# A wide causal attention phase whose mask and scale move to VectorE, and whose exponentials are eight per item on ScalarE with their sums

## The reference

```python
q = split_heads(x @ Wq)
k = split_heads(x @ Wk)
v = split_heads(x @ Wv)
q = apply_rope(q)
k = apply_rope(k)
sim = jnp.einsum('bid,bjd->bij', q, k) * scale
causal = jnp.tril(jnp.ones((t, t), dtype=bool))
sim = jnp.where(causal[None], sim, -jnp.inf)
attn = jax.nn.softmax(sim, axis=-1)
out = jnp.einsum('bij,bjd->bid', attn, v)
...
return out @ Wo + bo
```

## Time and profile before

| | |
|---|---|
| median of 3 runs | 1160.22 us (1157.81 to 1162.24) |
| the profiled execution | 1151.02 us, of which the span of the engines is 1149.2 us |
| wide attention phase in the span | about 594 to 1002 us |
| one block of it, at steady pace | 24.12 us, so 6.03 us an item |

### The profile page before, as it was taken

The page is one execution under the profiler, slowest core; times in us unless marked ns, Lnnn a source line. Parts: engine busy times, 40 slices in busy tenths (PEclk is TensorE's granted clock), DMA queues, the critical chain, the costliest instruction groups (busy, mean ns, idle before and its releaser), DMA issues. The chain is left out here.

```text
span 1149.2 us, 38657 instructions
## 1 busy us (share of the span) xinstructions
PE 993.0 (86%) x14756; PEld 799.4 (70%) x14759; DVE 846.6 (74%) x2027; ACT 588.4 (51%) x982; POOL 562.9 (49%) x705
## 2 busy tenths in 40 slices
PE   5999999999945799999937999999999999778554
PEld 2666666667632799999936888888888888655113
DVE  5878787888749344444418989999999998578676
ACT  3665656677730566666612444444444444366545
POOL 4232424353300533333126888888888877433104
PEclk9999999999965899999968999999999999955555
DMA  8200000000000111111130000000000000050002
GB/s 257 101 2 0 2 11 20 21 20 28 11 28 0 45 47 48 48 46 48 39 108 13 12 13 11 9 11 11 11 11 9 11 9 1 11 138 20 1 0 74
DMA packets 36984, 37.60 MB, mean 33 GB/s; under 512 B 7142, under 2 KB 31145, under 8 KB 36522
## 3 DMA queue, kind: packets, MB, share of 16 engines
q1 hardware_dynamic: 31690, 27.33, 7.9%
q0 software_dynamic: 4352, 8.92, 3.1%
q10 hardware_dynamic: 866, 0.33, 0.1%
HBM read 27.65 MB, written 8.91 MB: 32 GB/s over the span
## 5 line engine op out<-in xcount | busy, mean ns | idle before, releaser
L1283 POOL DMA_INDIRECT e_x<-xn_rows,e_where x72 | 68.2, 947 | 162.5 <-DVE e_where L1264 114.7
L360 POOL TENSOR_SCALAR n_KX<-n_KT,n_of_head 128x512 f32<-128x512 f32 x124 | 83.8, 697 | 122.1 <-ACT n_KT L601 85.2
L1253 DVE COPY e_y<-e_Y_ps 128x128 f32<-128x128 f32 x72 | 21.0, 292 | 112.5 <-PE e_Y_ps L1220 112.5
L760 DVE TENSOR_REDUCE n_row_max<-n_S_ps 128x16 f32<-128x1024 f32 x64 | 78.1, 1221 | 26.3 <-PE n_S_ps L451 26.3
L1440 POOL TENSOR_TENSOR a_E<-a_E,a_rsum 128x512 f32<-128x512 f32 x64 | 66.6, 1041 | 53.8 <-DVE a_rsum L1804 53.7
L665 ACT ACTIVATE n_ET<-n_ET_ps 128x1024 f32<-128x1024 f32 x64 | 65.5, 1023 | 46.5 <-PE n_ET_ps L461 45.8
L461 PEld LDWEIGHTS n_ET_ps<-ident,n_E 128*128 128x128 f32 x512 | 57.1, 142 | 34.9 <-issue 20.1
L764 DVE TENSOR_TENSOR n_E<-n_S_ps,n_row_max 128x1024 f32<-128x1024 f32 x64 | 78.4, 1225 | 2.9
L1210 PE MATMUL e_G_ps<-e_xT,e_gate_here 128*128 128x128 f32 x576 | 77.2, 278 | 0.0
L1210 PE MATMUL e_U_ps<-e_xT,e_up_here 128*128 128x128 f32 x576 | 76.9, 277 | 0.0
L1688 ACT ACTIVATE a_OT<-a_VQ_ps 128x512 f32<-128x512 f32 x64 | 38.2, 597 | 75.4 <-PE a_VQ_ps L1584 75.4
(11 more groups left out here) (280 smaller groups left out, 2674.3 us busy)
## 6 DMA issues: line engine op xcount, KB each, us to landing
slot_out<-e_y SPq DMA_DIRECT2D x72, 64.0 KB, 1.5
X<-in_x SPq DMA_DIRECT2D x8, 256.0 KB, 5.4
n_ctxT<-in_ctxT SPq DMA_DIRECT2D x8, 256.0 KB, 3.2
m_gate_w<-in_L_ffn_gate_w SPq DMA_DIRECT2D x1, 2048.0 KB, 7.4
m_up_w<-in_L_ffn_up_w SPq DMA_DIRECT2D x1, 2048.0 KB, 13.4
m_down_w<-in_L_ffn_down_w SPq DMA_DIRECT2D x1, 2048.0 KB, 17.7
xn_rows<-n_xn SPq DMA_DIRECT2D x8, 256.0 KB, 2.2
t_ctxT<-in_ctxT SPq DMA_DIRECT2D x8, 256.0 KB, 3.4
```

What stands on the lines that cost most here:

```text
L360: last = nc.gpsimd.tensor_scalar(KX[:, p, :, h * T:(h + 1) * T], src, of_head[:, h:h + 1], 1.0, ALU.mult, ALU.mult)
L760: nc.vector.tensor_reduce(row_max[:, u % 2, :], src, AX.X, ALU.max).then_inc(max_done, 1)
L1283: nc.gpsimd.indirect_dma_start(out=x[:, j, :], out_offset=None, in_=k.xn_rows, in_offset=bass.IndirectOffsetOnAxis(ap=where[:, j, :], axis ...
```

## The change

It does this in the wide attention phase alone:

- The eight constant matmuls are gone. VectorE multiplies the scores by 1/8 and adds a constant tile `future` (0 or -1e30) in one instruction (`mask_scores`, scalar_tensor_tensor) from PSUM into E, and then takes the negated row maximum `low` from E.
- ScalarE takes the exponentials in eight instructions per item, one for each head and half, 128x64 each, in place. `low` comes in as the per-row bias and the sum goes out as the accumulator output `row_sum`. The eight are spread over the step: two before evacuate_v and evacuate_e, two behind them, four behind the copy of the transposed input. The row sum on VectorE is gone.
- The weights are turned into bank 0 of the scores instead of the key bank, and behind project_q and project_v in TensorE's order. So scores(n+1) waits until evacuate_e(n-1) is done, and the transposed input goes to bank 1.
- The reciprocals of item n stand at the head of VectorE's step n, ahead of mask_scores(n+1), and normalise_e(n) at the head of GpSimd's step n (before, both were done for n+1 within step n). rotate_k runs for n+2 in place of n+3, ahead of rotate_q.
- One more constant tile of 64 KB is loaded, and the prologue's order follows.

The core of the diff (left out: the bank's new name, semaphores, the prologues, the constant):

```diff
                 for g in range(G):
                     if later(nxt, 2) and g == 3:
                         power(blk + 2)
-                    if g + 1 < G or nxt:
-                        normalise_e(*item_at(blk, g + 1))
+                    normalise_e(blk, g)
+                    if g + 2 < G or nxt:
+                        rotate_k(*item_at(blk, g + 2))
                     if g + 3 < G or nxt:
                         rotate_q(*item_at(blk, g + 3))
-                        rotate_k(*item_at(blk, g + 3))
...
                 n_ = blk * G + g
                 pe.wait_ge(rq_ready, n_ + 1)
                 if later(n_, 1):
-                    pe.wait_ge(d_ready, n_)
+                    pe.wait_ge(masked, n_)
+                if later(n_, 2):
+                    pe.wait_ge(et_ready, n_ - 1)
...
-                for h in range(GH):
-                    half = slice(64 * (h % 2), 64 * (h % 2) + 64)
-                    for b in range(2):
-                        nc.tensor.matmul(S_ps[64 * b:64 * b + 64, h, 0:P], k.causal_queries[half, 0:T], k.causal_keys[half, 0:P],
-                                         start=True, stop=False)
-                for a in range(2):
-                    for u in range(UB):
+                for u in range(UB):
+                    for a in range(2):
                         for b in range(2):
                             tok = slice((2 * b + u) * T, (2 * b + u + 1) * T)
                             for h in range(GH):
                                 rows = slice(32 * h, 32 * h + 32)
                                 mm = nc.tensor.matmul(S_ps[64 * b:64 * b + 64, h, u * T:(u + 1) * T], RQ[rows, g % 2, a, tok],
-                                                      RK[rows, g % 2, a, tok], start=False, stop=(a == 1 and u == UB - 1))
+                                                      RK[rows, g % 2, a, tok], start=(a == 0), stop=(a == 1))
                 mm.then_inc(s_ps, 1)
             def transpose_e(blk, g):
                 n_ = blk * G + g
-                pe.wait_ge(pk_ready, at_most_all(n_ + 3))
+                pe.wait_ge(masked, at_most_all(n_ + 2))
                 pe.wait_ge(en_ready, n_ + 1)
                 for h in range(GH):
-                    mm = nc.tensor.transpose(KE_ps[:, h * P:(h + 1) * P], E[:, g % 2, h * P:(h + 1) * P], k.ident[:])
+                    mm = nc.tensor.transpose(S_ps[:, 0, h * P:(h + 1) * P], E[:, g % 2, h * P:(h + 1) * P], k.ident[:])
                 mm.then_inc(et_ps, 1)
...
             def step(blk, prev, nxt):
                 for g in range(G):
                     if g + 1 < G or nxt:
                         scores(*item_at(blk, g + 1))
-                    transpose_e(blk, g)
                     if g + 3 < G or nxt:
                         project_q(*item_at(blk, g + 3))
                     if g + 1 < G or nxt:
                         project_v(*item_at(blk, g + 1))
+                    transpose_e(blk, g)
                     if g + 3 < G or nxt:
...
-            def exponentials(blk, g):
-                act.wait_ge(d_ready, blk * G + g + 1)
-                nc.scalar.activation(E[:, g % 2, :], E[:, g % 2, :], ACT.Exp, scale=SCALE).then_inc(e_ready, 1)
+            def exponentials(blk, g, heads):
+                n_ = blk * G + g
+                act.wait_ge(max_ready, n_ + 1)
+                if later(n_, 2):
+                    act.wait_ge(rsum_ready, n_ - 1)
+                for j in range(heads[0] * UB, (heads[-1] + 1) * UB):
+                    e = E[:, g % 2, j * T:(j + 1) * T]
+                    last = nc.scalar.activation(e, e, ACT.Exp, bias=low[:, g % 2, j:j + 1], accum_out=row_sum[:, g % 2, j:j + 1])
+                if heads[-1] == GH - 1:
+                    last.then_inc(e_ready, 1)
...
-                nc.scalar.activation(ET[:, g % 2, :], KE_ps[:], ACT.Copy).then_inc(et_ready, 1)
+                nc.scalar.activation(ET[:, g % 2, :], S_ps[:, 0, :], ACT.Copy).then_inc(et_ready, 1)
...
             def step(blk, p, prev, nxt):
                 for g in range(G):
                     if nxt == 3 and g == 0:
                         slots_of(blk + 3, 1 - p)
+                    if g + 1 < G or nxt:
+                        exponentials(*item_at(blk, g + 1), range(1))
+                        evacuate_v(*item_at(blk, g + 1))
                     evacuate_e(blk, g)
                     if g + 1 < G or nxt:
-                        exponentials(*item_at(blk, g + 1))
-                    if g + 1 < G or nxt:
-                        evacuate_v(*item_at(blk, g + 1))
+                        exponentials(*item_at(blk, g + 1), range(1, 2))
+                    if nxt and g == 0:
+                        evacuate_xT(blk + 1)
                     if nxt and g == 2:
                         keep_xT(blk + 1)
-                    if nxt and g == 0:
-                        evacuate_xT(blk + 1)
+                    if g + 1 < G or nxt:
+                        exponentials(*item_at(blk, g + 1), range(2, GH))
                     evacuate_o(blk, g)
...
-            def subtract_max(blk, g):
-
+                products(K_ps[:], PK).then_inc(pk_ready, 1)
+
+            def mask_scores(blk, g):
                 n_ = blk * G + g
                 dve.wait_ge(s_ps, n_ + 1)
-                src = S_ps[:, :, 0:P].rearrange("p h (u t) -> p h u t", t=T)
-                top = row_max[:, g % 2, :].rearrange("p (h u) -> p h u", u=UB)
-                nc.vector.tensor_reduce(top, src, AX.X, ALU.max).then_inc(max_ready, 1)
                 if later(n_, 2):
                     dve.wait_ge(et_ps, n_ - 1)
-                dve.wait_ge(max_ready, n_ + 1)
-                nc.vector.tensor_tensor(E[:, g % 2, :].rearrange("p (h u t) -> p h u t", u=UB, t=T), src,
-                                        top.unsqueeze(3).broadcast_to([P, GH, UB, T]), ALU.subtract).then_inc(d_ready, 1)
+                e = E[:, g % 2, :].rearrange("p (j t) -> p j t", t=T)
+                nc.vector.scalar_tensor_tensor(out=E[:, g % 2, :].rearrange("p (h k) -> p h k", h=GH), in0=S_ps[:, :, 0:P],
+                                               scalar=SCALE, in1=future[:].unsqueeze(1).broadcast_to([P, GH, P]),
+                                               op0=ALU.mult, op1=ALU.add).then_inc(masked, 1)
+                if later(n_, 2):
+                    dve.wait_ge(e_ready, n_ - 1)
+                dve.wait_ge(masked, n_ + 1)
+                nc.vector.tensor_reduce(low[:, g % 2, :], e, AX.X, ALU.max, negate=True).then_inc(max_ready, 1)
             def reciprocals(blk, g):
                 n_ = blk * G + g
                 dve.wait_ge(e_ready, n_ + 1)
-                nc.vector.tensor_reduce(row_sum[:, g % 2, :], E[:, g % 2, :].rearrange("p (j t) -> p j t", t=T), AX.X, ALU.add)\
-                    .then_inc(sum_ready, 1)
                 if later(n_, 2):
                     dve.wait_ge(en_ready, n_ - 1)
-                dve.wait_ge(sum_ready, n_ + 1)
                 nc.vector.reciprocal(rsum[:, g % 2, :], row_sum[:, g % 2, :]).then_inc(rsum_ready, 1)
...
             def step(blk, p, prev, nxt):
                 for g in range(G):
+                    reciprocals(blk, g)
                     if g + 1 < G or nxt:
-                        subtract_max(*item_at(blk, g + 1))
+                        mask_scores(*item_at(blk, g + 1))
                     if prev and g == 1:
                         add_residual(blk - 1)
                     if g + 3 < G or nxt:
                         products_q(*item_at(blk, g + 3))
-                    if g + 1 < G or nxt:
-                        reciprocals(*item_at(blk, g + 1))
-                    if g + 3 < G or nxt:
                         products_k(*item_at(blk, g + 3))
```

47 lines of the change are left out of this document (22 added, 25 removed).

## The result

The changed kernel takes 1190.8 us (median of 4 runs, 1188.42 to 1192.12) against 1160.4 us for the kernel before on the same chip: a ratio of 1.0271 (95% interval 1.0246 to 1.0296). It is slower by 30 us, and lies outside the predicted range.

A forecast was written before the change was run, and what follows sets the result against it. VectorE's list was taken as the bound before, then a two-item chain at 6.00 us an item against 6.03. 15 blocks at 0.0 each plus 2 took 1151.0 to 1153 us, a median near 1161; range 1142 to 1178.

The forecast's parts named there:

- The step that failed: On GpSimd: same instructions in another order, normalise_e still ending just ahead of the turning; counted as nothing.
- the "wrong" signs: Signs against the forecast: exponentials 0.24 apart, no TensorE gap before project_q, or the turning waiting for GpSimd's normalise_e.
- TensorE without a gap before project_q: On TensorE, a sign against the forecast: it would mean that evacuate_o is not late.
- The exponentials, e = 0.34: On ScalarE: e, the time between exponentials' starts, is 0.34 us, so eight take 2.7; no change, chance 0.38.
- the upper values of e: On ScalarE: exponentials start 0.34 or 0.43 us apart, expected if the accumulator output makes each two instructions.
- The chain of 24.1: Project_k through combine, mask, exponentials, evacuate_o, project_q: 12.00 us for two items; four passes laid out give 24.1 a block.
- TensorE stands still before project_q, 0.3 to 0.8 us in most passes: On TensorE, a sign for the forecast: idle time put down to evacuate_o, where before there was none.
- VectorE's busy time, to about 200 of 240: On VectorE, a sign for the forecast: busy time in 240 us falls from 229 to about 200.
- The mask, 0.72: On VectorE: multiplying the scores and adding the constant tile takes 0.72 us per item.
- sums for nothing, 1146: Rival on ScalarE: sums almost free, exponentials 0.24 apart, block 23.1 us, 1146 us; chance 0.33 for faster altogether.
- The non-overlapping accumulator: Rival on ScalarE: accumulator output a full instruction, e = 0.43, block about 25.2, 1179 us; chance 0.29 for slower altogether.
- the held mask: Rival on VectorE: GpSimd holds the mask up 0.5 us an item, block 25.1, about 1177 us; chance 0.03.

The follow-up runs named there:

- experiment 1: Changed kernel with GpSimd's gather moved between rotate_k and rotate_q instead of behind rotate_q: 1161.1 us, ratio 1.0029 to the kernel before.
- experiment 3: Kernel before with its gather moved ahead of normalise_e, behind the wait for the reciprocals, so that it lies on the scores: 1208.0 us, ratio 1.0419.
- experiments 2 and 4: Changed kernel, gathers of blocks 3 to 15 replaced by a GpSimd addition over 128x448 (1164.7 us), or the gather by a plain 64 KB load (1160.4 us).
- experiment 6: As experiment 1, but the exponentials have no accumulator output and the row sums are a constant 1: 1146.8 us, ratio 0.9883 to the kernel before.
- Experiments 10 to 12: On experiment 1: evacuate_o ahead of the last head's exponentials (ratio 1.0052); that plus reciprocals between mask and maximum (1.0083); those reciprocals alone (1.0091).
- experiment 7: As experiment 1, but one 128x512 exponential per item in place of eight, without sums, maximum unused: 1149.3 us, ratio 0.9909 to the kernel before.

## Why the prediction was wrong

**The step that failed** is "GpSimd has the same instructions in another order. [...] I count nothing." I had looked at GpSimd's load, and at whether normalise_e stays ahead of the turning. I had not asked what lies beside the gather on other engines, before and after. The same 0.98 us moved from the projections to the weighed values and the scores, and there the scores cost TensorE 0.66 to 1.26 us more in each pass, 3.6 a block. In experiment 1 the same four stretches, scores to project_q, are 1.2 us a block above 0.85, waiting for `evacuate_o`; the stop swallows these waits. Net it is 26.4 less 24.1, 2.3 us a block or 0.57 a pass, over 12 to 13 blocks: 28 to 30 us. Experiment 1 takes away 28 us by moving the gather alone, experiment 3 puts a loss into the kernel before by moving the gather, experiments 2 and 4 exclude GpSimd's load and a plain transfer. None of my rivals had it: the "wrong" signs that I listed were signs of the chain and of normalise_e. One of them, TensorE without a gap before project_q, did appear in the changed kernel, and not because `evacuate_o` was early but because the scores were late.

**The exponentials, e = 0.34**: right. They start 0.33 apart, 340 ns each:

```profile
849.23 0.34 ACT L1674 ACTIVATE a_E<-a_E,a_low 128x64 f32<-128x64 f32 x1
...
849.46 0.20 ACT L1674 ACTIVATION_READ_ACCUMULATOR a_E<-a_E,a_low 128x1 f32 x1
849.56 0.34 ACT L1674 ACTIVATE a_E<-a_E,a_low 128x64 f32<-128x64 f32 x1
```

And the sum is an instruction of its own, 192 ns, as the page VectorE: DVE Perf Modes of the Trainium skill (Two Vector instructions with no wait between them) has it for VectorE. By that alone I had called the upper values of e the likely ones; the trace shows that the accumulator read starts while the exponential is still in its tail, so it costs only 0.09 of start-to-start. The group of the window:

```profile
L1674 ACT ACTIVATION_READ_ACCUMULATOR a_E<-a_E,a_low 128x1 f32 x288 | 55.3, 192 | 0.0
```

Without the sums (experiment 6) the timeline counts four exponentials in 1.06 us, so 0.24 apart, the lower end of e as I had it:

```profile
841.63 1.06 ACT L1675 ACTIVATE a_E<-a_E,a_low 128x64 f32<-128x64 f32 x4
```

**The chain of 24.1**: the number came out, the terms not all. Experiment 1, which is the change with the gather out of the way, has 24.12, the ratio is 1.0029, and 1161.1 us against the predicted 1161. Its passes are 6.48, 5.64, 6.30 and 5.68 where I had 6.1, 6.0, 6.3 and 5.7: the pair adds up, the first two did not come out singly. The sum has 1.51 for `combine`. Experiment 1 has 0.61 in one pass (849.21), behind which the reciprocal waits 0.50 for the last exponential, and 1.26 to the reciprocal in the next:

```profile
850.32 0.20 DVE L1807 RECIPROCAL a_rsum<-a_row_sum 128x8 f32<-128x8 f32 x1 [0.50 <-ACT a_E L1674]
...
855.36 1.34 DVE L1742 SCALAR_TENSOR_TENSOR X<-a_expert_rows,gates,X 128x128 f32 x2
```

So the line that I summed is not what holds VectorE at 850.32, and that the total met 24.1 is in part luck. "The chain" was also too simple. Experiments 10 to 12 found two more lines within 3% of it, and experiment 7 a floor at 23.4. Cutting the one that I had summed brought nothing.

**TensorE stands still before project_q, 0.3 to 0.8 us in most passes**: half right. In experiment 1 it does so in every other pass, up to 0.7 us; in the changed kernel the stop had used it up. The view of waits of experiment 1 has VectorE's wait before the products of k too, as written:

```profile
DVE a_PK L1770 <- PE a_K_ps L1521: 24.9, 40, 0.9
...
PE a_VQ_ps L1513 <- ACT a_OT L1690: 9.6, 20, 0.7
```

**VectorE's busy time, to about 200 of 240**: 193 in experiment 1. It is 168 in the changed kernel, which runs fewer items in that time, and whose `combine` is short. **The mask, 0.72**: 0.69, and GpSimd does not hold it:

```profile
L1794 DVE SCALAR_TENSOR_TENSOR a_E<-a_S_ps,a_future 128x512 f32<-128x512 f32 x37 | 25.6, 691 | 35.0 <-PE a_S_ps L1554 35.0
...
L1742 DVE SCALAR_TENSOR_TENSOR X<-a_expert_rows,gates,X 128x128 f32 x36 | 10.9, 344 | 0.0
```

The other row there is the reason why misled me about `combine`. I took its 1.51 us as fixed. It is 0.34 us an instruction on average where it lies beside the gather, and 0.83 in the kernel before, where it lies beside rotate_q.

**The rivals**: sums for nothing, 1146, is what experiment 6 measured (1146.8). The non-overlapping accumulator and the held mask did not occur. The range of 1142 to 1178 was said to take in both ends of e, and the upper, 1179, lies just outside it. So most of what I had priced came out, and the 30 us lay in the term that I had set to zero.

What stays open is how a gather stops TensorE. The stop ends about 0.3 us after the gather's instruction (851.45 to 851.74), and the weighed values report late as well: `a_OT` starts 2.00 us after their start in place of 1.28, though their matmuls ran as always. Whether TensorE isn't given its instructions or can't signal was not separated, nor why the weighed values and the projections don't stop. The scores are its densest group, 64 matmuls in 0.85 us where the weighed values have 32 in 0.63; that this is the reason is not shown.

## What to carry to other kernels

When a change moves an instruction in an engine's order, it also moves what it lies beside: list for each moved instruction, DMA issues first, what the other engines do in that stretch, before and after. In these kernels a gather that started 1.5 us or more ahead of the scores cost them nothing. And where several lines of waiting are within 3% of each other, cutting one of them can show nothing but the next: sum all of them before moving work.

## What the runs showed of the hardware

- A gather issued by GpSimd (0.98 us) that lies on the scores (64 fp32 matmuls of 32x64) stops them from 0.6 to 1.0 us behind its start until 0.2 to 0.4 behind its end, and they take 0.66 to 1.26 us more. On the weighed values (64x64, 32 of them) and on matmuls of 128x128 and 128x256 no stop was seen, nor on the scores with a plain load (0.58 us) or an addition of GpSimd's (0.94 us) in its place.
- An exponential with an accumulator output is two instructions on ScalarE, 340 and 192 ns, and 0.33 us from one to the next; without it 0.24.
- VectorE's multiply-add of two SBUF tensors, 128x128, takes 344, 526, 833 or 1045 ns on average in four kernels, and a pair 0.61 to 2.92 us, by what GpSimd does beside it (703 against 571 ns where little more than GpSimd's instruction differed, experiments 2 and 4). The Trainium skill (VectorE: DVE Perf Modes, Two Vector instructions with no wait between them) says that the second SBUF input is read through an interface shared with GpSimd; it gives no price, and these are the prices here. The mask, with one input from PSUM, kept to 0.69.
